# First pass's channel product: contraction over 128 partitions with zero rows in place of 19 rows

## The chip, the cores and the metric

The kernel runs on one core of a Trainium2 chip, in one launch. The metric is the device time in microseconds (us). The engines of the core are TensorE (PE for its matmuls, PEld for its weight loads), VectorE (DVE), ScalarE (ACT), GpSimd (POOL) and SyncE (SP), whose only work here is to issue DMAs.

## The reference, cut to what matters

The input is 32 images of 8 channels and 64 x 64 points. Four blocks follow one another, each adding its result to its input: a cellular automaton (L0), a convolution on a sphere (L1), a spectral network (L2) and a second convolution on a sphere (L3). The change lies in L2 alone, which is:

```
x = x + _L2_conv_ref(_gn(x), ...)          # _gn: group norm, 4 groups

xg    = x.reshape(Bb, G, SC, Hh, Ww)                      # G = 4 groups of SC = 2 channels
gridb = broadcast(stack([gridx, gridy]), (Bb, G, 2, Hh, Ww))
h = concatenate([xg, gridb], axis=2)                      # 4 inputs to each group
h = _gconv1x1(h, fc0_w, fc0_b)                            # 4 groups x 10 = 40 channels
for i in range(4):
    h1 = _spectral_conv(h, sp_w1[i], sp_w2[i])            # rfft2, 24 x 12 modes mixed, irfft2
    h2 = _gconv1x1(h, w_w[i], w_b[i])
    h = h1 + h2
    if i < 3: h = _gswish(h, betas[i])
h = _gswish(_gconv1x1(h, fc1_w, fc1_b), betas[3])
return _gconv1x1(h, fc2_w, fc2_b)
```

All is float32. The line that matters is `h = _gconv1x1(h, fc0_w, fc0_b)`: 8 channels, two coordinates and a bias become 40 channels at every point.

## The kernel before, in words

`program` calls the stages one after another: group norm, the coupled map, the automaton, its gate, group norm, sphere, group norm, `spectral`, group norm, sphere. Each stage is a `Phase` that ends in a barrier of all engines, and no stage overlaps the next.

`spectral` begins with `spectral_layers` (phase `fno`). It makes four passes (`layer` 0 to 3, called the first to the fourth pass here) over 8 units (`u`). A unit is four images, as two halves (S2) of two images (B2). For each unit TensorE does, in the order in which it is written:

- `pointwise(layer, u, t)` for t = 0 to 15: the channel product. Each t makes four matmuls (L1230), one for each image row h, whose stationary operand is 128 points (2 images x 64 columns) and whose moving operand is the weights, 96 columns wide. In the first pass the stationary operand is `form_in[0:KX]` with KX = 19 partitions: 2 x 8 channels, two coordinates and a row of ones; the moving operand is `wz`, a table of 19 x 96. In the later passes both have 128 partitions, `chan` and `cols`. A float32 matmul leaves two records each for load and matmul in the trace, so 16 x 4 matmuls of a unit are 128 records. ScalarE takes each t out of PSUM (L1316), four PSUM banks deep.
- after t = 1, `forward_rows` of the unit before (L1267), and at the unit's end `forward_cols` (L1258, 8 groups of 5 matmuls, 80 records, all 128 partitions), whose groups VectorE copies out (L1397). From the second pass on, `inverse_rows` (L1243) stands between them.

After the 8 units `mix` (L1281) multiplies the modes by the spectral weights; it waits for modes that are read back from memory.

SyncE issues all DMAs on one queue in written order. Before the first product: `wz`, `load_x(0)`, which fills 16 partitions of `form_in`'s first buffer, `coords` (3 partitions), `fw`, betas, biases, `load_x(1)`, `coords` again, `fh`, `ih`, and behind a wait for a memset of VectorE (`set_up`) the table `point_w`. TensorE begins when all seven `tables` have landed. In the loop, unit n's last product (`z_done`) releases `load_x(n + 2)` and unit n's last activation releases the store of its result (2.5 MB, `form`); in units 6 and 7 `z_done` releases instead the tables `iw_t` and `load_unit`, which fill `form_in` for the second pass. The modes of unit n are stored (`scratch_modes`) once `forward_rows` is done. `form_in` has two buffers of 128 x 8192, one for even and one for odd units; in the first pass partitions 19 to 127 of it hold nothing that is read.

Of the kernel before, what the change touches and what calls it, by code (L numbers as in the profile page):

```python
# [13 lines left out]
B, C, H, W = 32, 8, 64, 64  # L14
# [5 lines left out]
LAYERS = 4  # L20
# [19 lines left out]
CS = CH * S2  # L40
PIX = B2 * W
# [106 lines left out]
def laid_out(inp):  # L148

    c = {}  # L150
    z = lambda *shape: np.zeros(shape, dtype=np.float32)
    col = lambda v, n: np.ascontiguousarray(np.tile(v, n).reshape(-1, 1))

    m = z(3, R1 + 2, C, R1, HID)
    for h in range(R1):
        for y in range(3):
            m[:, h + y, :, h, :] = inp["L0_conv_Wp"][:, :, y, :].transpose(2, 1, 0)
    c["nca_w"] = m.reshape(3 * (R1 + 2) * C, R1 * HID)
    m = z(R1, HID, R1, C)
    for h in range(R1):  # L160
        m[h, :, h, :] = inp["L0_conv_Wu"][:, :, 0, 0].T
    c["nca_u"] = m.reshape(R1 * HID, R1 * C)
    c["nca_bp"], c["nca_bu"] = col(inp["L0_conv_bp"], R1), col(inp["L0_conv_bu"], R1)
    m = z(R2 + 2, C, 3, 3, R2, C)
    w = inp["L0_conv_Wg1"].reshape(C, 3, C, 3, 3)
    for h in range(R2):
        for y in range(3):
            m[h + y, :, :, :, h, :] = w[:, :, :, y, :].transpose(2, 1, 3, 0)
    c["gate_w"] = m.reshape((R2 + 2) * C, 9, R2 * C)
    m = z(R2, C, R2, C)  # L170
    for h in range(R2):
        m[h, :, h, :] = inp["L0_conv_Wg2"][:, :, 0, 0].T
    c["gate_u"] = m.reshape(R2 * C, R2 * C)
    c["gate_b1"], c["gate_b2"] = col(inp["L0_conv_bg1"], R2), col(inp["L0_conv_bg2"], R2)
    for n in (1, 3):
        w = inp[f"L{n}_conv_weight"].reshape(C, C, 9).transpose(1, 0, 2)
        c[f"sph{n}_w"], c[f"sph{n}_b"] = np.ascontiguousarray(np.tile(w, (16, 1, 1))), col(inp[f"L{n}_conv_bias"], 13)

    m, m0 = z(CS, LAYERS, CS), z(KX, 96)
    for g in range(G):  # L180
        for t in range(S2):
            o = (g * S2 + t) * WID
            m0[t * C + 2 * g:t * C + 2 * g + 2, o:o + WID] = inp["L2_conv_fc0_w"][g, :, 0:SC].T
            m0[2 * C:2 * C + 2, o:o + WID] = inp["L2_conv_fc0_w"][g, :, SC:SC + 2].T
            m0[2 * C + 2, o:o + WID] = inp["L2_conv_fc0_b"][g * WID:(g + 1) * WID]
            for n in range(LAYERS):
                m[o:o + WID, n, o:o + WID] = inp["L2_conv_w_w"][n, g].T
    c["point_w"], c["fc0"] = m, m0
    c["w_bias"] = np.ascontiguousarray(inp["L2_conv_w_b"].T)
    betas = inp["L2_conv_betas"]  # L190
    m = np.ascontiguousarray(np.broadcast_to(betas[None, None, :, 0], (128, 3, LAYERS)).astype(np.float32))
    m[SB:128, 0], m[0:CH, 1], m[:, 2] = (np.repeat(betas.T, n, axis=0) for n in (S2 * WID, WID, FC))
    c["betas"] = m.reshape(128, 3 * LAYERS)
    m = z(LAYERS, 2, 4, 2, G, WID, XC, KY, G, WID)
    for half, name in enumerate(("L2_conv_sp_w1", "L2_conv_sp_w2")):
        w = inp[name].reshape(LAYERS, G, WID, WID, 4, XC, KY, 2).transpose(4, 7, 1, 0, 2, 5, 6, 3)
        for g in range(G):
            m[:, half, :, :, g, :, :, :, g, :] = w[:, :, g].transpose(2, 0, 1, 3, 4, 5, 6)
    c["mix_w"] = m.reshape(LAYERS, CHUNKS, 2 * CH, XC * KY, CH)
    m, m2 = z(CS, S2, 128), z(128, S2, 16)  # L200
    for g in range(G):
        f = slice(FC * g, FC * g + FC)
        for t in range(S2):
            o = (g * S2 + t) * WID
            m[o:o + WID, t, f] = inp["L2_conv_fc1_w"][g].T
            m2[f, t, t * C + 2 * g:t * C + 2 * g + 2] = inp["L2_conv_fc2_w"][g].T
    c["fc1"], c["fc2"], c["fc1_b"], c["fc2_b"] = m, m2, col(inp["L2_conv_fc1_b"], 1), col(inp["L2_conv_fc2_b"], 4 * S2)
    return c
# [804 lines left out]
KX = S2 * C + 3  # L1013
# [36 lines left out]
def spectral_layers(nc, k, xn2, form, modes, mixed, kept):  # L1050
# [4 lines left out]
    form_in, chan, cols, wsm, rates, dc, ih, unit_in = (kept[n] for n in ("form_in", "chan", "cols", "wsm", "rates", "dc", "ih", "unit_in"))  # L1055
    with Phase(nc, "fno") as ph:
# [2 lines left out]
        both, minus = ph.sb("both", [4 * NX, 20 * SB]), ph.sb("minus", [4 * NX, 20 * SB])  # L1059
        coef = ph.sb("coef", [4 * NX, CH // 2, 2 * SB])  # L1060
        fw, fh = ph.sb("fw", [128, 2 * SB]), ph.sb("fh", [128, 2, 4 * NX])
        wz = ph.sb("wz", [KX, 96])
        om1 = ph.sb("om", [CH, XC * 4 * B * KY])
        wt = ph.sb("wt", [2 * CH, WTS, XC * KY, CH])
        work = ph.sb("work", [128, 6, 3 * LAYERS])
# [1 line left out]
        pz = ph.ps("pz", [128, 4, NB])  # L1067
        pj, pw = ph.ps("pj", [128, 2, NB]), ph.ps("pw", [128, 2, NB])

        tables, iw_in, set_up, beta_in, step, scaled, filled = (ph.sem(n) for n in ("tables", "iw_in", "set_up", "beta_in", "step", "scaled", "filled"))  # L1070
        (z_done, a_out, turned, w_done, c_out, h_done, d_out, m_out, both_out, coef_in, j_done, j_out) = (ph.sem(n) for n in (
            "z_done", "a_out", "turned", "w_done", "c_out", "h_done", "d_out", "m_out", "both_out", "coef_in", "j_done", "j_out"))
# [14 lines left out]
        def om_tile(b, t, ri, v):  # L1087
            o = om(b)[:, t // 2, ri, :].rearrange("p (a v c y) -> p y a v c", v=2, c=B2, y=KY)
            return o[:, 6 * (t % 2):6 * (t % 2) + 6, :, v]

        def acc_tile(n, part):
            return pz[0:CH, n % 4, 0:384].rearrange("p (y r a c) -> p y r a c", y=6, r=2, c=B2)[:, :, part]

        with nc.Block() as block:
            @block.sync
            def _(sp):
                def load_x(u):
                    for t in range(S2):
                        sp.dma_start(form_in[t * C:t * C + C, u % 2, :].rearrange("p (h f) -> p h f", h=H),
                                     xn2[:, :, u * 4 * W + t * PIX:u * 4 * W + t * PIX + PIX].rearrange("h c f -> c h f")).then_inc(unit_in[u % 2], 16)  # L1100

                sp.dma_start(wz[:, :], k["fc0"]).then_inc(tables, 16)
                load_x(0)
                sp.dma_start(form_in[2 * C:KX, 0, :], k["coords"]).then_inc(tables, 16)
                sp.dma_start(fw[:, :], k["fw"]).then_inc(tables, 16)
                sp.dma_start(work[:, 0, :], k["betas"]).then_inc(beta_in, 16)
                sp.dma_start(wbias[:, :], k["w_bias"]).then_inc(beta_in, 16)
                load_x(1)
                sp.dma_start(form_in[2 * C:KX, 1, :], k["coords"]).then_inc(tables, 16)
                sp.dma_start(fh[:, :, :], k["fh"]).then_inc(tables, 16)  # L1110
# [27 lines left out]
                for layer in range(LAYERS):  # L1138
# [39 lines left out]
                    for n in range(CHUNKS + 2):  # L1178
                        m = layer * CHUNKS + n
# [20 lines left out]

            @block.gpsimd
            def _(pool):
                for n in range(LAYERS * UNITS):
                    if n:
                        pool.wait_ge(both_out, 64 * n)
                    pool.wait_ge(d_out, (n + 1) * NH)
                    nc.gpsimd.tensor_scalar(minus[:, :], both[:, :], -1.0, None, ALU.mult).then_inc(m_out, 1)  # L1207

            @block.tensor
            def _(pe):  # L1210
                pe.wait_ge(set_up, 2)
                pe.wait_ge(tables, 16 * 7)

                def pointwise(layer, u, t):
                    n = layer * UNITS + u
                    if t == 0:
                        if not layer:
                            pe.wait_ge(unit_in[u % 2], unit_loads(n))
                        else:
                            pe.wait_ge(j_out, (n - 8 + 1) * NJ)  # L1220
                            if u == 0:
                                pe.wait_ge(filled, 16 * layer)
                    if layer and t % 2 == 0:
                        pe.wait_ge(turned, (n - UNITS) * NT8 + t // 2 + 1)
                    if n * NZ + t >= 4:
                        pe.wait_ge(a_out, n * NZ + t - 3)
                    for m in range(4):
                        h = 4 * t + m
                        left = chan[:, h % 32 * PIX:(h % 32 + 1) * PIX] if layer else form_in[0:KX, u % 2, h * PIX:(h + 1) * PIX]
                        mm = nc.tensor.matmul(pz[:, t % 4, m * 96:(m + 1) * 96], left, cols[:, h * CS:h * CS + 96] if layer else wz[:, :],  # L1230
                                              start=m == 0, stop=True, skip_group_check=True)
                    mm.then_inc(z_done, 1)
# [113 lines left out]

            @block.vector
            def _(dve):
                nc.vector.memset(wsm[:, :, :], 0.0).then_inc(set_up, 1)
                nc.vector.memset(cols[:, COLS:COLS + 16], 0.0).then_inc(set_up, 1)  # L1350
                dve.wait_ge(beta_in, 32)
# [55 lines left out]
                for layer in range(LAYERS):  # L1407
# [12 lines left out]
                    for n in range(CHUNKS):  # L1420
                        m = layer * CHUNKS + n
                        for t in range(0, TILES, 2):
# [3 lines left out]
                            for ri, v, part, sign in PARTS:  # L1426
                                o, z = om_tile(m % 2, t, ri, v), acc_tile(m * TILES + t, part)
# [12 lines left out]
def unit_loads(n):  # L1440

    uses = n // 2 + 1
    return 32 * min(UNITS // 2, uses) + 48 * max(0, uses - UNITS // 2)
# [292 lines left out]
```

## Time and profile before

| | us |
|---|---|
| median of 3 runs | 3541.56 (3535.78 to 3544.45) |
| the profiled execution, its own time | 3535.98 |
| its span, first to last instruction | 3534.2 |
| TensorE busy | 2931.7 (83% of the span) |
| weight loads busy | 2234.9 (63%) |
| VectorE busy | 1844.6 (52%) |
| ScalarE busy | 1394.4 (39%) |
| GpSimd busy | 697.7 (20%) |
| mean granted TensorE clock | 0.870 of full speed |

A busy engine need not be at its peak: TensorE's busy time holds both what it does at the full granted clock (2.4 GHz, shown as 1.00) and what it does at the half (1.2 GHz, 0.50). The profile's line "PEclk" and the views by stretches show which. In a timeline, the number in brackets is the idle time before an instruction, with what ended it.

### The profile page before, as it was taken

The page shows a single profiled execution, that of the slowest core. Times are in us where ns is not written, and L with a number is a line of the kernel's source. Part 1 is how long each engine was busy: PE and PEld are TensorE (multiplying, and loading weights), DVE is VectorE, ACT ScalarE, POOL GpSimd, SP SyncE. Part 2 cuts the span into 40 slices and gives each one's busy share as a digit, 9 for nine tenths or more (in the row PEclk, how much of TensorE's full clock was granted, in tenths as well). Part 3 has the DMA queues.
Part 4 walks back from the last instruction along what each step waited for, and adds up shares of the span by engine and source line. Part 5 has one row for each costly group of instructions (what it writes and reads, how often), then busy time and mean ns, then how long its engine had stood idle before and what let it go on. Part 6 is the DMA issues. An engine that isn't in the chain of part 4 may idle for free. (4 is left out here: it accounts for less than half of the span.)

```text
span 3534.2 us, 44282 instructions
## 1 busy us (share of the span) xinstructions
PE 2931.7 (83%) x16948; PEld 2234.9 (63%) x16948; DVE 1844.6 (52%) x2409; ACT 1394.4 (39%) x2331; POOL 697.7 (20%) x651
## 2 busy tenths in 40 slices
PE   0799997969484499968997899978997799999758
PEld 0344441136253499867996899967996788787535
DVE  6888773335536111144553545444553478888643
ACT  1877773422122111143332433343332466565422
POOL 3888400013110000000000000000000044444410
PEclk9999998989797576758998699958998599999879
DMA  8200014579334544666776587766776724332123
GB/s 209 56 23 0 23 37 140 156 156 201 97 93 134 106 94 95 156 205 149 192 168 176 160 204 161 179 192 149 193 167 177 165 49 77 65 63 51 59 89 92
DMA packets 343979, 437.88 MB, mean 124 GB/s; under 512 B 260410, under 2 KB 302010, under 8 KB 317394
## 3 DMA queue, kind: packets, MB, share of 16 engines
q1 hardware_dynamic: 343304, 430.36, 50.4%
q0 software_dynamic: 496, 5.01, 0.4%
q8 instruction: 127, 2.08, 0.3%
q14 instruction: 52, 0.43, 0.0%
HBM read 258.55 MB, written 168.58 MB: 121 GB/s over the span
## 5 line engine op out<-in xcount | busy, mean ns | idle before, releaser
L1026 DVE STREAM_TRANSPOSE spec_chan<-spec_form_in 128x1024 f32<-128x1024 f32 x256 | 492.2, 1946 | 65.8 <-PE fno_pz L1230 65.7
L1316 ACT ACTIVATE fno_act<-fno_pz 128x320 f32<-128x320 f32 x512 | 223.8, 437 | 700.6 <-PE fno_pz L1230 700.5
L1397 DVE COPY fno_wfreq<-fno_pw 128x240 f32<-128x240 f32 x256 | 97.7, 395 | 596.8 <-PE fno_pw L1258 594.8
L1207 POOL TENSOR_SCALAR fno_minus<-fno_both 96x960 f32<-96x960 f32 x32 | 83.4, 2605 | 1549.4 <-DVE fno_both L1405 1549.4
L1230 PEld LDWEIGHTS fno_pz<-spec_cols,spec_chan 128*128 128x128 f32 x3072 | 348.2, 192 | 12.3 <-issue 9.5
L1230 PE MATMUL fno_pz<-spec_cols,spec_chan 128*128 128x96 f32 x3072 | 350.0, 275 | 2.0 <-ACT spec_cols L1324 2.0
L1281 PE MATMUL fno_pz<-fno_act,fno_wt 80*40 80x64 f32 x2304 | 248.7, 308 | 108.2 <-DMA fno_act<-scratch_modes 101.3
L1258 PE MATMUL fno_pw<-fno_fw,fno_act 128*128 128x96 f32 x2560 | 323.5, 288 | 14.5 <-DVE fno_wfreq L1397 8.7
L1258 PEld LDWEIGHTS fno_pw<-fno_fw,fno_act 128*128 128x128 f32 x2560 | 311.4, 203 | 27.7 <-DVE fno_wfreq L1397 15.6
L1281 PEld LDWEIGHTS fno_pz<-fno_act,fno_wt 80*40 80x40 f32 x2304 | 245.6, 184 | 113.6 <-issue 113.5
L1531 POOL TENSOR_TENSOR head_hact_lo<-head_hact,head_hact_hi 128x512 fp32r<-128x512 f32 x128 | 227.8, 1783 | 403.5 <-DVE head_hact_hi L1678 403.5
L574 PE MATMUL cml_acc<-cml_logis,cml_mats 128*128 128x512 f32 x480 | 247.0, 596 | 56.2 <-DVE cml_logis L531 56.2
L1243 PE MATMUL fno_pj<-spec_ih,fno_coef 96*48 96x128 f32 x1920 | 224.6, 280 | 43.9 <-DMA fno_coef<-scratch_mixed 43.9
L576 PE MATMUL cml_acc<-cml_moved,cml_mats 128*128 128x512 f32 x480 | 246.7, 595 | 9.5 <-ACT cml_moved L497 9.5
L1243 PEld LDWEIGHTS fno_pj<-spec_ih,fno_coef 96*48 96x48 f32 x1920 | 206.9, 126 | 58.1 <-DMA fno_coef<-scratch_mixed 44.6
L1230 PE MATMUL fno_pz<-fno_wz,spec_form_in 19*128 19x96 f32 x1024 | 182.6, 362 | 52.2 <-DMA spec_wsm<-table_point_w 52.2
L1230 PEld LDWEIGHTS fno_pz<-fno_wz,spec_form_in 19*128 19x128 f32 x1024 | 179.5, 274 | 58.1 <-issue 57.4
L1628 ACT ACTIVATE head_hact<-head_pw,head_b,spec_rates 128x512 f32<-128x512 f32 x256 | 189.3, 778 | 45.5 <-PE head_pw L1572 23.6
L574 PEld LDWEIGHTS cml_acc<-cml_logis,cml_mats 128*128 128x128 f32 x480 | 91.7, 191 | 171.5 <-issue 114.6
L539 DVE SCALAR_TENSOR_TENSOR cml_grid<-cml_acc,cml_drive 128x512 f32<-128x512 f32 x224 | 154.4, 690 | 76.2 <-PE cml_acc L576 76.0
L1324 ACT ACTIVATE spec_cols<-fno_pj 48x512 f32<-48x512 f32 x240 | 141.6, 590 | 125.3 <-PE fno_pj L1243 125.3
L496 ACT ACTIVATE cml_moved<-cml_logis 64x496 f32<-64x496 f32 x240 | 148.1, 617 | 90.2 <-DVE cml_logis L544 88.8
(155 smaller groups left out, 4614.8 us busy)
## 6 DMA issues: line engine op xcount, KB each, us to landing
scratch_form<-fno_act SPq DMA_DIRECT2D x32, 2560.0 KB, 17.0
spec_form_in<-scratch_form SPq DMA_DIRECT2D x64, 1024.0 KB
fno_act<-scratch_modes SPq DMA_DIRECT2D x128, 180.0 KB
nca_win<-scratch_xnp SPq DMA_DIRECT2D x66, 329.7 KB
fno_coef<-scratch_mixed SPq DMA_DIRECT2D x48, 360.0 KB, 10.8
spec_form_in<-scratch_form SPq DMA_DIRECT2D x32, 512.0 KB
fno_wt<-table_mix_w SPq DMA_DIRECT2D x32, 450.0 KB, 10.3
gn_x<-scratch_x SPq DMA_DIRECT2D x12, 1024.0 KB
```

Source lines behind the costliest of these rows:

```text
L496: nc.scalar.activation(bj(moved[0:64, t, :])[:, :, 0:J - 1], bj(logis[0:64, t, :])[:, :, 1:J], ACT.Copy).then_inc(moved_ready, 1)
L539: nc.vector.scalar_tensor_tensor(out=grid[:, t % 4, :], in0=acc[:, t % BANKS, :], scalar=FLOOR, in1=drive[:, t, :], op0=ALU.max, op1=ALU.a ...
L574: nc.tensor.matmul(acc[:, t % BANKS, :], mats[:, 0, c].rearrange("p s h -> p (s h)"), logis[:, t, :], start=True, stop=False)
L576: nc.tensor.matmul(acc[:, t % BANKS, :], mats[:, 1, c].rearrange("p s h -> p (s h)"), moved[:, t, :], start=False, stop=True).then_inc(sum ...
L1026: return nc.vector.transpose(chan[:, to * TR * PIX:(to + 1) * TR * PIX].rearrange("p (h q w) -> p h q w", h=TR, q=4), src)
L1230: mm = nc.tensor.matmul(pz[:, t % 4, m * 96:(m + 1) * 96], left, cols[:, h * CS:h * CS + 96] if layer else wz[:, :], start=m == 0, stop=Tr ...
L1243: mm = nc.tensor.matmul(pj[0:SB, t % 2, m * 2 * H:(m + 1) * 2 * H], coef[:, g * WID + i, sub * SB:(sub + 1) * SB], ih[:, :], start=m == 0, ...
L1258: mm = nc.tensor.matmul(pw[:, t % 2, m * 2 * SB:(m + 1) * 2 * SB], act_b[:, n % 2, c0:c0 + 2, :].rearrange("p c h -> p (c h)"), fw[:, :], ...
L1281: mm = nc.tensor.matmul(pz[0:CH, n % 4, j * 64:(j + 1) * 64], wt[:, m % WTS, t // 2 * KY + y, :], rows[:, t // 2, :, :].rearrange("p r (a ...
L1316: nc.scalar.activation(act_b[:, n % 2, :, 4 * t:4 * t + 4], z, ACT.Silu if layer else ACT.Copy).then_inc(a_out, 1)
L1531: nc.gpsimd.tensor_tensor(hpart[1][:, n % 2, 1, :], hact[:, n % 2, 1, :], hpart[0][:, n % 2, 1, :].bitcast(F32), ALU.subtract).then_inc(f_ ...
L1628: nc.scalar.activation(hact[:, e % 2, s, :], pw[:, s, :], ACT.Silu, scale=rates[:, 0, 2, 3:4], bias=b1[:, :]).then_inc(f_act, 1)
```

## The change

The weights `wz` and their table `fc0` get 128 rows in place of 19, rows 19 to 127 zero. The stationary operand of the first pass takes all 128 partitions of `form_in`. So that those partitions hold zeros and not what lay there, both buffers are cleared first: in each, VectorE the lower half of the columns, GpSimd the upper, with a semaphore each (`blank_half`, `blank`). SyncE waits for both halves of buffer 0 before `load_x(0)` and of buffer 1 before `load_x(1)`; TensorE waits for them too. VectorE's two memsets stand ahead of its memset of `wsm`, which gives `set_up`. Nothing of the later passes is changed.

```diff
-    m, m0 = z(CS, LAYERS, CS), z(KX, 96)
+    m, m0 = z(CS, LAYERS, CS), z(128, 96)
...
-        wz = ph.sb("wz", [KX, 96])
+        wz = ph.sb("wz", [128, 96])
...
+        blank, blank_half = ph.sem("blank"), ph.sem("blank_half")
...
                 sp.dma_start(wz[:, :], k["fc0"]).then_inc(tables, 16)
+                sp.wait_ge(blank, 1)
+                sp.wait_ge(blank_half, 1)
                 load_x(0)
...
+                sp.wait_ge(blank, 2)
+                sp.wait_ge(blank_half, 2)
                 load_x(1)
...
             @block.gpsimd
             def _(pool):
+                for b in range(2):
+                    nc.gpsimd.memset(form_in[:, b, H * PIX // 2:H * PIX], 0.0).then_inc(blank, 1)
+                    pool.wait_ge(blank, b + 1)
...
             def _(pe):
                 pe.wait_ge(set_up, 2)
+                pe.wait_ge(blank, 2)
+                pe.wait_ge(blank_half, 2)
                 pe.wait_ge(tables, 16 * 7)
...
-                        left = chan[:, h % 32 * PIX:(h % 32 + 1) * PIX] if layer else form_in[0:KX, u % 2, h * PIX:(h + 1) * PIX]
+                        left = chan[:, h % 32 * PIX:(h % 32 + 1) * PIX] if layer else form_in[:, u % 2, h * PIX:(h + 1) * PIX]
...
             def _(dve):
+                for b in range(2):
+                    nc.vector.memset(form_in[:, b, 0:H * PIX // 2], 0.0).then_inc(blank_half, 1)
                 nc.vector.memset(wsm[:, :, :], 0.0).then_inc(set_up, 1)
```

## Rows read from the trace of the kernel before

**Rows 1.** The page: busy time of each engine; granted clock in 40 slices.

```profile
PE 2931.7 (83%) x16948; PEld 2234.9 (63%) x16948; DVE 1844.6 (52%) x2409; ACT 1394.4 (39%) x2331; POOL 697.7 (20%) x651
...
PEclk9999998989797576758998699958998599999879
```

**Rows 2.** TensorE's groups by shape: count, busy us, mean ns, idle before.

```profile
L1230 PE MATMUL fno_pz<-spec_cols,spec_chan 128*128 128x96 f32 x3072 | 350.0, 275 | 2.0 <-ACT spec_cols L1324 2.0
...
L1230 PE MATMUL fno_pz<-fno_wz,spec_form_in 19*128 19x96 f32 x1024 | 182.6, 362 | 52.2 <-DMA spec_wsm<-table_point_w 52.2
```

**Rows 3.** Timeline of TensorE, first pass: start us, us, line, operation, count.

```profile
1193.16 27.59 PE L1230 MATMUL fno_pz<-fno_wz,spec_form_in 19*128 19x96 f32 x128 [52.18 <-DMA spec_wsm<-table_point_w]
...
1221.28 11.52 PE L1258 MATMUL fno_pw<-fno_fw,fno_act 128*128 128x96 f32 x80 [0.53 <-ACT fno_act L1316]
...
1258.07 11.89 PE L1258 MATMUL fno_pw<-fno_fw,fno_act 128*128 128x96 f32 x80 [0.53 <-ACT fno_act L1316]
...
1485.03 11.09 PE L1258 MATMUL fno_pw<-fno_fw,fno_act 128*128 128x96 f32 x80 [0.53 <-ACT fno_act L1316]
```

**Rows 4.** Stretches of 10 us: busy of each engine, PEclk, DMA share, GB/s.

```profile
1210.00:1220.00 10.00, 10.00 (x49) 10.00 (x49) 0.00 (x0) 2.62 (x6) 0.00 (x0) 0.50 0.00 0
...
1250.00:1260.00 10.00, 9.47 (x45) 9.23 (x45) 0.00 (x0) 2.19 (x5) 0.00 (x0) 0.50 0.06 14
...
1270.00:1280.00 10.00, 10.00 (x67) 7.74 (x67) 1.71 (x3) 2.66 (x7) 2.60 (x1) 1.00 0.28 116
```

**Rows 5.** Timeline of ScalarE, first pass twice, then second pass.

```profile
1279.07 0.44 ACT L1316 ACTIVATE fno_act<-fno_pz 128x320 f32<-128x320 f32 x1 [0.46 <-PE fno_pz L1230]
...
1285.84 0.44 ACT L1316 ACTIVATE fno_act<-fno_pz 128x320 f32<-128x320 f32 x1 [1.27 <-PE fno_pz L1230]
...
1630.69 0.44 ACT L1316 ACTIVATE fno_act<-fno_pz 128x320 f32<-128x320 f32 x1 [0.46 <-PE fno_pz L1230]
```

**Rows 6.** Timeline of TensorE in the second pass, and VectorE in the first.

```profile
1654.73 1.95 PE L1230 MATMUL fno_pz<-spec_cols,spec_chan 128*128 128x96 f32 x16
...
1656.52 3.39 PE L1267 MATMUL fno_pw<-fno_wfreq,fno_fh 128*96 128x480 f32 x8
...
1659.74 12.64 PE L1230 MATMUL fno_pz<-spec_cols,spec_chan 128*128 128x96 f32 x112
...
1231.72 0.41 DVE L1397 COPY fno_wfreq<-fno_pw 128x240 f32<-128x240 f32 x1 [0.71 <-PE fno_pw L1258]
```

**Rows 7.** Stretches of 3 us: TensorE busy (instructions), PEclk, DMA share, GB/s.

```profile
1537.00:1540.00 3.00, 3.00 (x31) 0.50 0.02 9
...
1612.00:1615.00 3.00, 3.00 (x16) 0.50 0.00 0
...
1615.00:1618.00 3.00, 3.00 (x27) 0.94 0.00 0
```

**Rows 8.** Timeline before the first product: VectorE and SyncE's queue.

```profile
1157.52 0.33 DVE L1349 MEMSET spec_wsm<- 128x320 f32 x1 [5.84 <-PEq L234]
...
1160.80 5.44 SPq L1099 DMA_DIRECT2D spec_form_in<-scratch_xn  x2
...
1175.09 0.74 SPq L1113 DMA_DIRECT2D spec_wsm<-table_point_w  x1
```

**Rows 9.** Groups by shape: the large memsets of VectorE and GpSimd.

```profile
L639 DVE MEMSET nca_out<- 24x4224 f32 x1 | 3.6, 3578 | 0.8 <-issue 0.8
...
L457 POOL MEMSET cml_moved<- 128x8192 f32 x1 | 7.0, 6961 | 0.0
```

**Rows 10.** The pass's end: stretches of 3 us, then timeline rows.

```profile
1472.00:1475.00 3.00, 3.00 (x16) 0.50 1.35 155
...
1475.00:1478.00 3.00, 3.00 (x16) 0.50 0.31 29
...
1484.53 0.34 SPq L1155 DMA_DIRECT2D spec_form_in<-table_iw_t  x1
...
1529.55 38.80 PE L1281 MATMUL fno_pz<-fno_act,fno_wt 80*40 80x64 f32 x360 [29.48 <-DMA fno_act<-scratch_modes]
```

## The prediction

> **What bounds the kernel now.** I read the page first: TensorE is busy 83% of the span, no other engine over 52%, and the line of granted clocks falls to 5, 6 and 7 tenths in the slices from about 1150 to 1590 us, while it is mostly 8 or 9 elsewhere [rows 1]. Next the groups by shape. The same line, L1230, has two: with 19 partitions the mean matmul takes 362 ns, with 128 partitions 275 ns, though both load 128 columns of weights and stream 96 [rows 2]. The narrow one does not need more work; it runs at another clock. The stretches show it: at 1210 us and at 1250 us TensorE is busy 10.00 and 9.47 of 10 us at a granted clock of 0.50, which is 1.2 GHz; at 1270 us, after `forward_cols` with its 128 partitions, it is 1.00, 2.4 GHz [rows 4]. ScalarE's timeline gives the price: one tile of four products per 0.44 + 0.46 = 0.90 us just after `forward_cols`, one per 0.44 + 1.27 = 1.71 us from about 1282 us on, and again 0.90 us in the second pass at the full clock [rows 5]. So the first pass is TensorE bound (its idle time there is 0.53 us a unit), and much of it is at half clock. The reader should see that the engine was fully busy before the clock fell, and that only the shape of the work distinguishes the stretches.
>
> **The change part by part.**
>
> 1. *The product itself.* 512 matmuls get 128 partitions in place of 19. The 19-partition tile takes 0.90 us at the full clock and the 128-partition tile of the second pass takes 0.90 us too [rows 5], so the wider contraction costs nothing by itself at equal clock. Its worth is what the clock does. I take it that the clock then behaves as in the second pass: same two shapes, 128*128 and 128x96, 275 ns a matmul [rows 2], and there 112 records take 12.64 us without a slow tile [rows 6].
>
> The rule that speaks against this is in the Trainium skill, "TensorE: Matmul & The Clock Gate", Part 1, "What's actually happening": it says that the gate is set by how busy TensorE has been recently. And its Part 3 and the table under "Why this matters for your kernels" know a short contraction only as unused array, which takes the same time. By that rule nothing changes in the clock here, and the sum would be the start's cost alone. The trace disagrees with it as a complete rule: busy 10.00 of 10 us, clock 0.50 [rows 4].
>
> 2. *Unit 0.* Now 27.6 us for 16 tiles at 1.71 us [rows 3, 5]. TensorE will still start at the half clock, after the idle wait. The nearest bounds for how long: in the second pass the clock rises in the stretch that begins at 1615 us, seven microseconds after the first matmul at 1608.5 [rows 7]; at best it is at once. I take three tiles, 5.1 us, as 128 columns by 128 partitions fill more of the array than that stage's 96 by 48: 3 x 1.71 + 13 x 0.894 = 16.7 us (0.894 is 12.64 / 14 tiles less the overlap of the last matmul). Gain 10.9 us; bounds 10.1 (four slow tiles) and 13.3 (none).
>
> 3. *Units 1 to 7.* From the first `forward_cols` at 1221.28 to the eighth at 1485.03 are seven equal rounds, 263.75 us, 37.68 each [rows 3]. A round at the full clock: the idle 0.53; eight groups of `forward_cols` at 0.41 + 0.71 = 1.12 us, 8.93 in all [rows 6]; two tiles 1.79, `forward_rows` 3.22 and fourteen tiles 12.57, from the starts 1654.73, 1656.52 and 1659.74 and the last row's 12.64 less 0.07 by which the next begins before its end [rows 6]. Sum 27.0 us. Gain 7 x 10.6 = 74.5 us. About 8 us of each 10.6 are tiles, 2.5 are the first groups of `forward_cols`, which now run slow because the clock was down when they began (11.5 to 11.9 us against 8.9) [rows 3]. If the clock rises and falls as before, only less, half of it is left. Nothing else in the round needs more than 27.0 us: ScalarE needs 0.44 of each 0.90 us, and the DMA share between 1210 and 1280 us is 0.00, 0.06 and 0.28 in the stretches shown [rows 4].
>
> 4. *The last `forward_cols`* gains 2.2 us (11.09 to 8.9) [rows 3], which I count at nothing: behind it TensorE waits 29.48 us for modes read back from memory [rows 10], and those stand in SyncE's queue behind unit 7's tables, loads and store (6.5 MB by the shapes in the code), which are issued from 1484.53 on and not sooner for a faster `forward_cols`.
>
> 5. *DMA at the end of the pass.* Unit 6's tables, `load_unit` and store keep the DMA engines busy until about 1475.5 (share 1.35, then 0.31) [rows 10]. Unit 7's follow at 1484.53, nine microseconds later. With a round 10.6 us shorter they would be issued at about 1472.4 of the old time, 3.1 us before the engines are free. From that issue to the mix are 45.0 us (1484.53 to 1529.55), all DMA [rows 10], so I charge 3.1 us; bounds 0 and 10, the whole of the last round's gain.
>
> 6. *The start.* TensorE starts at 1193.16, when the last table lands, after 52.18 us idle [rows 3]. Before it SyncE's queue is full: the second `load_x` took 5.44 us to issue [rows 8]. Each half of a buffer is 4096 columns. VectorE's memset of 4224 columns took 3578 ns, so 3.5 us; GpSimd's of 8192 took 6961 ns, so 3.5 us [rows 9]. `load_x(0)` starts that much later and everything behind it too; the second buffer's halves are clear at 7 us, when `load_x(1)` could hardly have been issued anyway. `wsm`'s memset moves from 1157.52 to about 1164.5, still 10 us before its DMA is issued at 1175.09 [rows 8]. The wider `wz` adds 42 KB. Price 3.6 us. A gain is excluded, since the memsets stand ahead of the first load and remove nothing. Above: if the two engines' memsets run one after the other, the first buffer is clear at 7 us and the second at 14, and the start is 10 to 14 us late. The three waits of TensorE and the two new semaphores I take as nothing; they are met long before 1193.
>
> The Trainium skill, "GPSIMD Engine Reference", 1. Specifications, says that GpSimd's SBUF interfaces are shared with VectorE and contended in some of VectorE's modes. No row here shows two memsets side by side; by that rule the start would go by the upper bound just given.
>
> Sum: -10.9 - 74.5 + 3.1 + 3.6 = -78.7 us. On the profiled execution's own 3535.98 us that is 3457. That execution is 5.6 us below the median of the three runs, 3541.56; from the median it is 3463. I give 3461, as the next median may lie anywhere between. From the bounds the gain is 74.5 + 10.1 - 10 - 14 = 61 to 74.5 + 13.3 = 88 us, so 3448 to 3481.
>
> **The rivals.**
>
> *A. Products of zeros don't keep the clock* (the change doesn't do what it says). All 109 added partitions hold zeros in both operands. If the chip grants its clock by what is switched or multiplied, the pass stays as it is and only the start's cost remains: 3541.56 + 3.6 = 3545, within what a measurement can't tell from no change. For it: every row at the full clock has real data in at least one operand. Against it: code and rows together show mostly zero weights elsewhere at a full clock (the coupled map's band tables, in slices 3 to 6 at 9 tenths) [rows 1]. Chance 0.13.
>
> *B. The clock follows busy time alone*, the page's rule: as A, 3545. Against it stands 0.50 at 10.00 of 10 us, and `mix` too, with 80 x 40 of the array in use, at 0.50 while busy 3.00 of 3 us, whereas `inverse_rows`, 96 x 48, is lifted from 0.50 to 0.94 by as full an engine [rows 7]. Chance 0.03.
>
> *C. The clock rises, but something takes part of it back*: the modes' small DMAs, the store, or a clock that still falls in some units. Half of term 3 gone gives 3461 + 37 = 3498; a quarter 3480. For it: the pass then moves the same bytes in 70% of the time. Against it: the low DMA shares. Chance 0.12.
>
> *D. Slower.* No help from the clock, and the start pays in full: VectorE and GpSimd clear one after the other, each buffer at its turn, and `load_x(1)` with all that is queued behind it in SyncE's order waits until 14 us: 3541.56 + 14 = 3556. It decides against the kernel as soon as A or B holds and the delay of the first product exceeds 10.6 us (0.3% of the time). Chance 0.04.
>
> The forecast has the remaining 0.68.
>
> **How the numbers follow.** A change under 0.3%, 10.6 us, is what a measurement of this kernel can't tell from none. Faster: forecast and C, 0.80. Same: A, B, 0.16. Slower: D, 0.04. The forecast's own range is 3448 to 3481; reaching into C, 3444 to 3494 leaves out the 0.2 of A, B, D, and a far end of C.
>
> **What would show each step.** Granted clock 1.00 in 10 us stretches of the whole pass but its first microseconds; ScalarE's tiles at 0.90 us with no 1.71 after the first few; rounds of 27.0 us between `forward_cols`; the first product 3.6 us later after the phase's start; 45 to 48 us from the last product to the mix. The prediction is wrong if the clock falls to 0.50 within a unit's products, or if TensorE gains idle time in the rounds.

## The result, and the profile after

The changed kernel takes 3455.04 us (median of four runs, 3449.89 to 3464.63), the kernel before 3538.74 (now four runs, 3535.78 to 3544.45). The ratio is 0.9775, with a 95% interval of 0.9753 to 0.9797. The forecast was 3461 us. A second measurement later gave 3459.5 us and a ratio of 0.978 (0.9758 to 0.9802): faster than before again, though this interval alone does not exclude a gain a little under 2%.

The page's line of engines and its line of granted clocks, to be set against [rows 1]:

```profile
PE 2845.4 (82%) x16948; PEld 2153.2 (62%) x16948; DVE 1844.4 (53%) x2411; ACT 1394.5 (40%) x2331; POOL 704.3 (20%) x653
...
PEclk9999998989879599759996799959997699999879
```

TensorE is busy 86 us less for the same 16948 instructions, and the slices from the fourteenth on, which read 5, 7, 6, 7, now read 5, 9, 9, 7; the last of them holds the wait before the mix and the mix's beginning. The groups by shape (count, busy us, mean ns, idle before) answer to [rows 2]:

```profile
L1240 PE MATMUL fno_pz<-spec_cols,spec_chan 128*128 128x96 f32 x3072 | 350.0, 275 | 2.0 <-ACT spec_cols L1334 2.0
...
L1240 PE MATMUL fno_pz<-fno_wz,spec_form_in 128*128 128x96 f32 x1024 | 118.9, 278 | 56.9 <-DMA spec_wsm<-table_point_w 56.9
...
L1268 PE MATMUL fno_pw<-fno_fw,fno_act 128*128 128x96 f32 x2560 | 303.4, 277 | 14.4 <-DVE fno_wfreq L1409 8.5 <-ACT fno_act L1326 5.8
```

The first pass's product had a mean of 362 ns with 19 partitions and has 278 ns with 128, beside the second pass's 275. The third row is `forward_cols`, whose code is untouched. Before, its row was:

```profile
L1258 PE MATMUL fno_pw<-fno_fw,fno_act 128*128 128x96 f32 x2560 | 323.5, 288 | 14.5 <-DVE fno_wfreq L1397 8.7 <-ACT fno_act L1316 5.8
```

It is busy 20 us less, as in the first pass it no longer begins at a low clock: 9.17 us in each unit, before 11.09 to 12.24.

TensorE's timeline of the first pass (start us, us, line, operation, count), against [rows 3, 6, 10]:

```profile
1204.86 16.73 PE L1240 MATMUL fno_pz<-fno_wz,spec_form_in 128*128 128x96 f32 x128 [56.89 <-DMA spec_wsm<-table_point_w]
...
1222.11 9.17 PE L1268 MATMUL fno_pw<-fno_fw,fno_act 128*128 128x96 f32 x80 [0.53 <-ACT fno_act L1326]
...
1231.12 1.95 PE L1240 MATMUL fno_pz<-fno_wz,spec_form_in 128*128 128x96 f32 x16
...
1232.90 3.39 PE L1277 MATMUL fno_pw<-fno_wfreq,fno_fh 128*96 128x480 f32 x8
...
1236.12 12.64 PE L1240 MATMUL fno_pz<-fno_wz,spec_form_in 128*128 128x96 f32 x112
...
1249.29 9.17 PE L1268 MATMUL fno_pw<-fno_fw,fno_act 128*128 128x96 f32 x80 [0.53 <-ACT fno_act L1326]
...
1412.40 9.17 PE L1268 MATMUL fno_pw<-fno_fw,fno_act 128*128 128x96 f32 x80 [0.53 <-ACT fno_act L1326]
...
1459.89 30.97 PE L1291 MATMUL fno_pz<-fno_act,fno_wt 80*40 80x64 f32 x288 [34.36 <-DMA fno_act<-scratch_modes]
```

Unit 0 takes 17.25 us with its idle 0.53, before 28.12. The seven rounds from 1222.11 to 1412.40 are 27.18 us each, before 37.68 on average. Each consists of the pieces that the second pass had shown: 1.95, 3.39 and 12.64 us. The stretches of 10 us (busy of each engine, PEclk, DMA share, GB/s), against [rows 4]:

```profile
1200.00:1210.00 10.00, 5.14 (x26) 5.18 (x27) 0.77 (x4) 0.88 (x2) 0.00 (x0) 0.52 0.51 93
...
1210.00:1220.00 10.00, 10.00 (x92) 10.00 (x92) 0.00 (x0) 4.99 (x12) 0.00 (x0) 1.00 0.01 2
...
1320.00:1330.00 10.00, 10.00 (x92) 10.00 (x91) 0.00 (x0) 4.89 (x12) 1.30 (x1) 1.00 0.34 63
...
1380.00:1390.00 10.00, 9.47 (x85) 9.31 (x84) 1.26 (x4) 2.62 (x6) 0.00 (x0) 1.00 0.59 120
```

TensorE starts at 0.50 and has 1.00 within its first unit; then no stretch of the pass's products is below 1.00. In 10 us it now gets through 92 records, before 49.

The start, all engines (against [rows 8, 9]). "SPq" is SyncE issuing a DMA:

```profile
1164.35 0.33 SPq L1103 DMA_DIRECT2D fno_wz<-table_fc  x1
...
1164.36 7.08 POOL L1209 MEMSET spec_form_in<- 128x4096 f32 x2 [87.09 <-POOLq L234]
...
1165.28 3.47 DVE L1360 MEMSET spec_form_in<- 128x4096 f32 x1 [6.61 <-PEq L234]
...
1168.84 0.78 SPq L1100 DMA_DIRECT2D spec_form_in<-scratch_xn  x2
...
1169.56 3.47 DVE L1360 MEMSET spec_form_in<- 128x4096 f32 x1 [0.80 <-issue]
...
1173.11 4.31 SPq L1100 DMA_DIRECT2D spec_form_in<-scratch_xn  x2
```

GpSimd's two memsets take 7.08 us, VectorE's 3.47 us each, at the same time. `load_x(0)` is issued 4.5 us after `wz`, before 0.3; the first product comes 40.51 us after `wz`, before 35.79.

The pass's end, SyncE's queue (against [rows 10]):

```profile
1384.72 0.34 SPq L1160 DMA_DIRECT2D spec_form_in<-table_iw_t  x1
...
1404.44 7.18 SPq L1174 DMA_DIRECT2D scratch_modes<-fno_both  x1
...
1414.08 0.85 SPq L1160 DMA_DIRECT2D spec_form_in<-table_iw_t  x1
```

Unit 6's load begins at 1384.72; one store of its modes takes 7.18 us to issue, before 3.28, and unit 7's are issued at 1414.08, 2.2 us after its last product allowed it (0.04 us before). The DMA engines' busy share from 1400 to 1420 us is 1.01 and 1.16. From that product to the mix are 48.0 us, before 45.1.

### The profile page after: what moved, and what is told of

The parts are those of the page before. It is cut to its first block and busy times, and to the rows that moved or that the text cites. A ratio compares the mean times of both kernels' runs of the same rounds, so it can differ in the third digit from the quotient of the medians.

```text
span 3462.8 us, 44290 instructions
## 1 busy us (share of the span) xinstructions
PE 2845.4 (82%) x16948; PEld 2153.2 (62%) x16948; DVE 1844.4 (53%) x2411; ACT 1394.5 (40%) x2331; POOL 704.3 (20%) x653
## 5 line engine op out<-in xcount | busy, mean ns | idle before, releaser
L1291 PE MATMUL fno_pz<-fno_act,fno_wt 80*40 80x64 f32 x2304 | 248.1, 310 | 112.3 <-DMA fno_act<-scratch_modes 107.4
L1268 PE MATMUL fno_pw<-fno_fw,fno_act 128*128 128x96 f32 x2560 | 303.4, 277 | 14.4 <-DVE fno_wfreq L1409 8.5
L1268 PEld LDWEIGHTS fno_pw<-fno_fw,fno_act 128*128 128x128 f32 x2560 | 291.4, 192 | 26.9 <-DVE fno_wfreq L1409 15.4
L544 DVE SCALAR_TENSOR_TENSOR cml_logis<-cml_grid 128x512 f32<-128x512 f32 x224 | 171.1, 769 | 0.0
L576 PEld LDWEIGHTS cml_acc<-cml_moved,cml_mats 128*128 128x128 f32 x480 | 91.6, 191 | 126.6 <-issue 87.3
## 6 DMA issues: line engine op xcount, KB each, us to landing
fno_coef<-scratch_mixed SPq DMA_DIRECT2D x48, 360.0 KB, 10.9
```

Source lines behind the costliest of these rows:

```text
L544: nc.vector.scalar_tensor_tensor(out=logis[:, t, :], in0=grid[:, t % 4, :], scalar=-1.0, in1=grid[:, t % 4, :], op0=ALU.add, op1=ALU.mult) ...
L576: nc.tensor.matmul(acc[:, t % BANKS, :], mats[:, 1, c].rearrange("p s h -> p (s h)"), moved[:, t, :], start=False, stop=True).then_inc(sum ...
L1268: mm = nc.tensor.matmul(pw[:, t % 2, m * 2 * SB:(m + 1) * 2 * SB], act_b[:, n % 2, c0:c0 + 2, :].rearrange("p c h -> p (c h)"), fw[:, :], ...
L1291: mm = nc.tensor.matmul(pz[0:CH, n % 4, j * 64:(j + 1) * 64], wt[:, m % WTS, t // 2 * KY + y, :], rows[:, t // 2, :, :].rearrange("p r (a ...
```

## The experiments

Each is the changed kernel with one edit, but for the last two: the changed kernel as it is, and two edits together. Those with a ratio were timed several times beside the kernel before on the same chip; of the runs with 32, 64 and 96 partitions and the mix with 80 x 64 there is one time and its trace, and what is read from them is the trace.

**Fewer partitions: 32, 64, 96.** In all three the clearing, waits and tables stay.

```diff
-  form_in[:, u % 2, h * PIX:(h + 1) * PIX]   ...  wz[:, :]
+  form_in[0:K, u % 2, h * PIX:(h + 1) * PIX] ...  wz[0:K, :]      # K = 32, 64, 96
```

> The changed kernel with one thing different: the first pass contracts over partitions 0 to 31 of the cleared buffer (and rows 0 to 31 of the weights), not 0 to 127. All clearing and waiting stays. Theory (the granted clock follows how much of the array the matmuls use, here partitions times loaded columns, and not what the values are): 32 x 128 is about as much as the 96 x 48 of inverse_rows, which is lifted to the full clock in the kernel before, so the clock may hold; rounds between 27.2 us (holds) and 37.7 us (falls as with 19 rows), time 3455 or 3530. Rival (only the number of partitions counts): 32 is far below the 80 of the mix, which stays at half clock, so rounds of 37.7 us and about 3538 us.

> As the run with 32 partitions, with 64. Theory (used part of the array): clock 1.00 through the products, rounds of 27.2 us, time about 3455 us. Rival (number of partitions alone): 64 is below the 80 of the mix, which stays at 0.50, so rounds of 37.7 us and about 3538 us.

> As the run with 32 partitions, with 96. Both theories (used part of the array, or number of partitions alone): clock 1.00, rounds of 27.2 us, about 3455 us, as inverse_rows with 96 partitions is at the full clock. A clock that falls here would mean that only all 128 partitions do it.

Measured: 3543.85 us with 32, 3530.79 with 64, 3468.57 with 96. With 32 partitions, TensorE's timeline:

```profile
1205.48 27.59 PE L1240 MATMUL fno_pz<-fno_wz,spec_form_in 32*128 32x96 f32 x128 [57.25 <-DMA spec_wsm<-table_point_w]
...
1251.54 21.43 PE L1240 MATMUL fno_pz<-fno_wz,spec_form_in 32*128 32x96 f32 x112
```

Unit 0 takes 27.59 us as with 19, fourteen later tiles 21.43 us against 12.64 at the full clock; rounds average 37.68, as with 19. With 64 partitions, stretches of 10 us (busy of each engine, PEclk, DMA share, GB/s):

```profile
1230.00:1240.00 10.00, 10.00 (x67) 7.64 (x66) 2.73 (x7) 0.88 (x2) 0.00 (x0) 1.00 0.67 167
...
1250.00:1260.00 10.00, 9.51 (x45) 9.27 (x44) 0.00 (x0) 2.63 (x6) 0.00 (x0) 0.50 0.01 2
```

The clock is 1.00 after `forward_cols` and back at 0.50 with TensorE busy 9.51 of 10 us: 64 partitions do not hold it, and rounds average 36.79. Unit 0 takes 27.59 us here too. With 96 partitions, the timeline and the stretches:

```profile
1199.27 27.59 PE L1240 MATMUL fno_pz<-fno_wz,spec_form_in 96*128 96x96 f32 x128 [57.01 <-DMA spec_wsm<-table_point_w]
...
1244.65 12.64 PE L1240 MATMUL fno_pz<-fno_wz,spec_form_in 96*128 96x96 f32 x112
...
1271.84 12.64 PE L1240 MATMUL fno_pz<-fno_wz,spec_form_in 96*128 96x96 f32 x112
```

```profile
1210.00:1220.00 10.00, 10.00 (x49) 10.00 (x48) 0.00 (x0) 2.45 (x6) 0.00 (x0) 0.50 0.01 2
...
1250.00:1260.00 10.00, 9.47 (x85) 9.31 (x84) 0.41 (x1) 3.93 (x9) 0.00 (x0) 1.00 0.40 83
```

Here is the surprise. All of unit 0 runs at half clock, 27.59 us, which 96 partitions do not lift. After the first `forward_cols` (128 partitions) the clock is 1.00 and stays there: fourteen tiles in 12.64 us. The first round is 30.44 us, as its `forward_cols` starts at the half clock and takes 12.43 us; the six after it are 27.18 to 27.19. That makes 13.6 us more than in the changed kernel's trace (10.3 in unit 0, 3.3 in that round), and the one time, where 3455 was expected, is 13.5 us above the changed kernel's median. So for this product three things can be read: with 19, 32 and 64 partitions the clock falls, 96 hold it, 128 also lift it. My theory of the used area is refuted: 64 x 128 falls, though `inverse_rows` with 96 x 48, a smaller area, is lifted [rows 7]. The rival, the number of partitions, is borne out in its order. It is not the whole either: 96 partitions lift the clock in `inverse_rows` and not here. The two stages differ in moving columns as well, 128 in `inverse_rows` and 96 here (the mix has 64), and no run varied them. A rule that counts partitions together with the columns moved in a given time is a rival that no run here tests.

**The start alone.**

```diff
-  form_in[:, ...]  wz[:, :]
+  form_in[0:KX, ...]  wz[0:KX, :]          # KX = 19, everything else as in the changed kernel
```

> The changed kernel's clearing, waits and 128-row table, but the product contracts over the 19 partitions as before: the cost of the start alone. Theory: the clock falls as before, rounds of 37.7 us, and the first product comes 4.7 us later than before, as in the changed kernel's trace (40.5 against 35.8 us after the first DMA of the phase): 3538.7 + 4.7 = 3543 us, ratio to before 1.001. Rival (clearing the buffer or something else in the change than the contraction moves the clock): about 3455 us. The prediction's upper bound for the start: 14 us, 3553 us.

Measured: 3540.73 us, ratio to before 1.0005 (0.9992 to 1.0017). Its timeline:

```profile
1199.11 27.59 PE L1240 MATMUL fno_pz<-fno_wz,spec_form_in 19*128 19x96 f32 x128 [56.78 <-DMA spec_wsm<-table_point_w]
...
1227.22 12.51 PE L1268 MATMUL fno_pw<-fno_fw,fno_act 128*128 128x96 f32 x80 [0.53 <-ACT fno_act L1326]
...
1494.08 12.21 PE L1268 MATMUL fno_pw<-fno_fw,fno_act 128*128 128x96 f32 x80 [0.53 <-ACT fno_act L1326]
```

Unit 0 is 27.59 us again and the rounds average 38.12 (1227.22 to 1494.08), so it is the contraction and nothing else in the change that moves the clock. (Here too a round is either 36.8 or about 39.9 us; this trace has three of the long ones, the one of before has two.) The first product came 40.40 us after `wz` was issued, 4.6 more than before. The time of the whole cannot tell these 4.6 us from none; the traces can, as all eight profiles with this start have 39.5 to 40.9 us there, against 35.8 in the one of before.

**An earlier first product.** What needs no cleared buffer goes ahead in SyncE's queue, `load_x(1)` to its end, and `wsm`'s memset goes first on VectorE.

```diff
   sp.dma_start(wz[:, :], k["fc0"])
+  betas, w_bias; wait set_up, point_w; fw; fh; ih        # moved up, none needs form_in
   sp.wait_ge(blank, 1); sp.wait_ge(blank_half, 1)
   load_x(0)
   coords into buffer 0
-  fw; betas; w_bias
   sp.wait_ge(blank, 2); sp.wait_ge(blank_half, 2)
-  load_x(1)
   coords into buffer 1
-  fh; ih; wait set_up, point_w
+  load_x(1)
```

> The changed kernel with SyncE's first DMAs in another order: what needs no cleared buffer (betas, biases, point_w, fw, fh, ih) goes before the first load_x, and load_x(1) goes last, behind both coords; wsm is cleared first on VectorE. Theory (the first product waits for everything in SyncE's queue, load_x(1) among it, and the clearing leaves the DMA engines idle meanwhile): the first product comes some 12 to 16 us earlier than in the changed kernel (40.5 us after the first DMA there), rounds stay 27.2 us, 3455 - 14 = 3441 us, ratio to the changed kernel 0.996. Rival (the DMA engines' work up to the first product is what bounds it, and is only reordered): within 3 us of the changed kernel.

Measured: 3448.12 us, ratio to before 0.9739 (0.9723 to 0.9756). The timeline of its start:

```profile
1159.62 0.33 SPq L1103 DMA_DIRECT2D fno_wz<-table_fc  x1
...
1164.45 0.78 SPq L1100 DMA_DIRECT2D spec_form_in<-scratch_xn  x2
...
1169.02 2.10 SPq L1100 DMA_DIRECT2D spec_form_in<-scratch_xn  x2
...
1183.86 16.32 PE L1240 MATMUL fno_pz<-fno_wz,spec_form_in 128*128 128x96 f32 x128 [40.62 <-DMA spec_form_in<-table_coords]
```

The first product comes 24.24 us after `wz`, 16.3 earlier, on the wait for `coords` (40.62 us idle before, 56.89 in the changed kernel). The rounds stay 27.18 and the wait from the last product to the mix 47.9, so from `wz` to the mix are 278.8 us, 16.7 less than in the changed kernel (295.5). The median moved by only 7 to 11 us (from 3455.0 and 3459.5) where 14 were expected; what took the rest isn't shown, and stages outside the pass differ by as much from run to run.

**The same idea in the mix.** The weights get 128 partitions with zero rows, the modes' buffer is read over 128. SyncE waits for the clearing before it loads the mix's weights; the first product still comes 39.7 us after `wz`.

```diff
-  wt = ph.sb("wt", [2 * CH, WTS, XC * KY, CH])
+  wt = ph.sb("wt", [128, WTS, XC * KY * CH + pad])       # cleared once by GpSimd, rows 0:80 loaded
-  act_b[0:2 * CH, ...]
+  act_b[:, ...]                                          # rows 80:128 hold old activations
-  matmul(pz[0:CH, ...], wt[:, m % WTS, ...], rows[:, ...])
+  matmul(pz[0:cols, ...], wt[0:K, m % WTS, at:at + cols], rows[0:K, ...])   # K, cols = 128, 40
```

> The changed kernel with the same idea applied to the mix (80 x 40, half clock in all four passes): the weights tile gets 128 partitions, rows 80 to 127 zero, and the moving operand takes all 128 partitions of the buffer in which the modes lie, whose upper rows hold old activations. Theory (the number of partitions in use decides the clock, whatever they hold and however few columns are loaded): the clock rises to 1.00 a few us into each mix, and the tile's 1.28 us falls to what VectorE and ScalarE need, 1.71 us for every two tiles, 0.86 each; 48 tiles a pass, 4 passes, up to 192 x 0.42 = 80 us less, part of it lost to DMA waits in the mix and to a slow start: 3455 - 55 = 3400 us, between 3375 and 3430. Rival (used area of the array, partitions times loaded columns, decides): 128 x 40 = 5120 is above the 96 x 48 that is lifted, so it too expects a rise; it is told apart by the next run. Rival (the mix is bound by its DMAs or by VectorE and ScalarE): within 10 us of 3455.

> The changed kernel, its mix with 80 partitions as before but 64 loaded columns in place of 40 (the 24 extra are the next weights; what they give is not read). Theory (number of partitions decides): granted clock stays 0.50 in the mix, tiles 1.28 us, about 3455 us. Rival (used area of the array decides): 80 x 64 = 5120 is above the 96 x 48 = 4608 of inverse_rows, which is lifted, so the clock rises to 1.00 in the mix and the time falls as in the run with 128 partitions.

Measured: with 128 x 40 3445.71 us, ratio to before 0.9741 (0.9723 to 0.9758), which just meets the changed kernel's 0.9775 (0.9753 to 0.9797). The mix's group by shape, all four passes, in the changed kernel and with this edit:

```profile
L1291 PE MATMUL fno_pz<-fno_act,fno_wt 80*40 80x64 f32 x2304 | 248.1, 310 | 112.3 <-DMA fno_act<-scratch_modes 107.4 <-issue 4.9
...
L1294 PE MATMUL fno_pz<-fno_act,fno_wt 128*40 128x64 f32 x2304 | 200.8, 259 | 146.9 <-DMA fno_act<-scratch_modes 105.8 <-issue 27.1 <-DVE spec_cols L1448 8.3
```

Stretches of 6 us within the first mix of this run (busy of PE, PEld, DVE, ACT, POOL, then PEclk, DMA share, GB/s):

```profile
1458.00:1464.00 6.00, 6.00 (x78) 6.00 (x77) 5.78 (x14) 5.87 (x14) 0.00 (x0) 1.00 0.35 104
...
1470.00:1476.00 6.00, 3.04 (x36) 2.71 (x35) 4.66 (x12) 4.70 (x12) 0.00 (x0) 1.00 0.77 244
...
1482.00:1488.00 6.00, 4.24 (x43) 4.19 (x43) 2.00 (x6) 2.65 (x7) 0.00 (x0) 0.72 0.79 248
```

The clock came, the time did not. The clock is 1.00 in most stretches from 1458 us on, and 0.72 in two, with waits of TensorE in or before them. TensorE's busy time in the mix fell from 248.1 to 200.8 us, but its idle time before it rose from 112.3 to 146.9. From the first mix's start to the next `inverse_rows` it went from 79.4 to 75.6 us. What ends VectorE's waits for its output buffers in the first mix, in the changed kernel (first two rows) and now (us in total, times, longest):

```profile
DVE spec_cols L1445 <- DMA scratch_mixed<-spec_cols: 4.0, 2, 3.1
...
DVE fno_om L1445 <- DMA scratch_mixed<-fno_om: 1.0, 1, 1.0
...
DVE spec_cols L1448 <- DMA scratch_mixed<-spec_cols: 10.1, 3, 4.0
...
DVE fno_om L1448 <- DMA scratch_mixed<-fno_om: 9.4, 3, 4.1
```

VectorE waits 19.5 us for stores of mixed modes to leave its two output buffers, where it waited 5.0 in the changed kernel and 9.9 in the one before. And in the first full stretch, before those waits, VectorE and ScalarE are busy 5.78 and 5.87 of 6 us. So the mix had two bounds close under TensorE's, these two engines and its DMAs, and the rival that named them was right. I had expected 55 us, 3375 to 3430, and got 9 to 14.

With 80 x 64 (the second kernel of this edit: K = 80, cols = 64, pad = 24) it took 3449.28 us in one run, and the clock in the mix is as before at full activity (columns as above):

```profile
1476.00:1482.00 6.00, 6.00 (x59) 6.00 (x59) 4.82 (x12) 4.22 (x11) 0.00 (x0) 0.50 0.76 269
```

It is 0.50 in every such stretch of the first mix, though 80 x 64 is more area than 96 x 48. The group is 248.6 us busy, as with 40 columns. That is the second refutation of the area. The one time is 6 us under the changed kernel's median and 0.6 under the fastest of its nine runs; one run shows no gain.

**Again, and both.**

> The changed kernel itself, timed beside the next one on the same chip. Theory: 3455 us, ratio to before 0.9765 within 0.002, the mean of its own first measurement (0.9775, 0.9753 to 0.9797).

> Both edits together: the early order of the first DMAs and the mix over 128 partitions. Theory (they act in different stretches and add up; 16 us earlier first product, 9 us in the mixes): 3455 - 12 - 9 = 3434 us, ratio to before 0.970, faster than both kernels. Rival (the earlier first product is given back at the pass's end, where unit 7's DMAs wait for unit 6's): not below 3445 us.

Measured: the changed kernel 3459.5 us, 0.978 (0.9758 to 0.9802); both edits together 3434.21 us (3424.86 to 3437.99), 0.9707 (0.969 to 0.9724), as summed. The agreement within a microsecond is luck, as the early order alone had come 7 us short of its own sum. Its first product comes at 24.5 us, its mix takes 202.6 us of TensorE. It beats the kernel before by 2.9% and the changed one, timed beside it, by 25 us.

## Why the prediction was right

The sum was -78.7 us. The terms, each against the two profiled executions:

| step | forecast | measured |
|---|---|---|
| unit 0 | -10.9 | -10.9 (28.12 to 17.25) |
| seven rounds | -74.5 (27.0 each) | -73.5 (27.18 each) |
| DMA at the pass's end | +3.1 | +3.0 (44.5 to 47.5, from `forward_cols` to the mix) |
| start | +3.6 | +4.7 (35.79 to 40.51) |
| sum | -78.7 | -76.7 |
| spans of the two profiles | | -71.4 |

The four steps add up to -76.7 us, 2 from the forecast sum, and the medians differ by 83.7. The spans of the two profiled executions differ by only 71.4, because the phase began 7.0 us later in the one after (`wz` issued at 1164.35 against 1157.37), after code that is the same in both kernels, and what follows the mix's start was 1.7 us shorter. The nine profiles of the experiments have that point between 1153.6 and 1164.6 us. This spread of some 10 us, from stages that the change does not touch, is larger than the error of any term, and no term of mine stood for it. That the median came within 6 us of 3461 is in part this spread.

*The product and the clock.* Right: the pass behaves as the second pass, with the rates read there. The order of the argument is what carried it: the narrow product was at half clock while busy 10.00 of 10 us [rows 4], and the same line with 128 partitions was not, in the second pass.

*The rounds.* They were not "seven equal rounds": from the `forward_cols` starts of before, five took 36.8 us and two 39.9, as the clock fell at different points of the unit. The mean, 37.68, is what the sum used, so the term stands.

*Unit 0.* Some three slow tiles, as taken, which is luck in part: in the six profiles with 128 partitions unit 0's products take 16.2 to 17.4 us, and the clock rises 3.6 to 6.1 us after the first of them. The estimate's reason, the filled area, was wrong, as the run with 96 partitions shows: more area than `inverse_rows` and no lift at all.

*DMA at the pass's end.* The mechanism was right: SyncE is still held up by unit 6's DMAs when unit 7's are allowed, and issues them 2.2 us late. The agreement of 3.1 with 3.0 is luck. 1472.4 does not follow from the numbers given: 1484.53 less 10.6 is 1473.9, 1.6 us before the engines are free. The last round of before was one of the long ones, and shortened by 12.7 us.

*The start.* The lower end of the range held. GpSimd and VectorE cleared side by side, 7.08 us for two and 3.47 us for one. The Trainium skill, "GPSIMD Engine Reference", 1. Specifications, names contention where VectorE runs in a 2-port mode or reads two SBUF inputs. A memset reads none, so that the upper bound followed "by that rule" was read into it; the two engines' float32 memsets showed no contention here. Of the extra 1.1 us, 0.9 is VectorE beginning that much after GpSimd; the rest is less than the 1.4 us by which this start differs between profiles.

*The rivals.* A, that products of zeros don't keep the clock: refuted by 1.00 from a few microseconds into unit 0 to the pass's last product, with 109 zero partitions in both operands. B, busy time alone: refuted by the runs with 32 and 64 partitions, equally busy and at 0.50. That rule is from the Trainium skill, "TensorE: Matmul & The Clock Gate", Part 1; where page and runs differ, the runs decide. C, something takes part back: only the 3.0 us charged. D, slower, needed A or B; the start alone is 1.0005 (0.9992 to 1.0017).

## What to carry to other kernels

Where TensorE is busy all the time and the granted clock is at its half, look at how many partitions the matmuls contract over. Rows of zeros cost TensorE nothing here (0.90 us a tile with 19 and with 128 partitions, at the full clock) and can be worth its full clock. In this product 96 partitions were enough to hold it and only 128 lifted it, so pad to all 128. But the rows must be cleared, and that goes in front of the first load: order the queue so that the first product waits for nothing else. Before doing the same elsewhere, find the bound that lies next: in the first pass it was at least 10 us a round away; in the mix VectorE, ScalarE and the stores took over after 4 us of 79.

## What the runs showed of the hardware

- In one and the same product the granted clock went by the partitions contracted over, and busy time alone did not decide it. 19, 32 and 64 partitions let it fall from 1.00 to 0.50 (rounds of 37.7, 37.7 and 36.8 us), 96 held it (27.2 us) but left unit 0 at 0.50 for 27.59 us, and 128 lifted it 3.6 to 6.1 us after the first product, in six profiles.
- Zeros did not hinder it: with 109 of 128 partitions zero in both operands it was 1.00, and a tile took 0.90 us as in the second pass.
- In the mix, 80 partitions stayed at 0.50 with 40 and with 64 loaded columns, so loaded columns did not lift it; 128 x 40 had 1.00 for most of the first mix. Why 96 partitions lift it in `inverse_rows` (48 loaded and 128 moving columns) and not in the product (128 loaded and 96 moving) stays open.
- Holding and lifting came apart: with 96 partitions the product ran at the full clock behind `forward_cols`, but did not reach it by itself. Whether one rule gives both isn't shown; at the full clock the same work passes in half the time (92 records in 10 us against 49).
- GpSimd's and VectorE's memsets of 128 x 4096 float32 columns ran side by side at 3.5 us each.
